# A deep factorization machine on one core: TensorE signals the use of gates once per job and each tile once when it is begun

## The reference, cut to what matters

```python
sp_emb = emb_tables[fidx, sp_input]           # 2048 samples x 26 fields, rows of 32 out of 26 tables of 12500 rows
lin_vals = lin_tables[fidx, sp_input, 0]      # one more value per lookup
lin_output = ds_input @ lin_w.T + lin_b + jnp.sum(lin_vals, axis=1, keepdims=True)
s = jnp.sum(sp_emb, axis=1)
bi_pooled = 0.5 * (s * s - jnp.sum(sp_emb * sp_emb, axis=1))
x = jnp.concatenate([bi_pooled, ds_input], axis=1)      # 2048 x 45
h = jax.nn.relu(x @ w1.T + b1)                          # 45 -> 256
h = jax.nn.relu(h @ w2.T + b2)                          # 256 -> 128
out = jax.nn.sigmoid(h @ fw.T + fb + lin_output)
```

## Time and profile before

| | |
|---|---|
| time before, 3 runs | 456.66, 459.72, 461.10 us, median 459.72 |
| span of the profiled execution, first to last instruction | 459.0 us (its own time beside the span is not shown) |
| TensorE matmuls busy | 406.9 us (89%) |
| VectorE busy | 331.9 us (72%) |
| GpSimd busy | 283.8 us (62%) |
| ScalarE busy | 258.8 us (56%) |

### The profile page before, as it was taken

How to read it: one execution, slowest core, us unless ns; L and a number is a source line. 1 busy time by engine, 2 the same in 40 slices (tenths; PEclk the granted TensorE clock), 3 DMA queues, 4 the chain that set the end, 5 groups by cost and what they waited for, 6 DMA issues and landing times.

```text
span 459.0 us, 5550 instructions
## 1 busy us (share of the span) xinstructions
PE 406.9 (89%) x1798; PEld 335.6 (73%) x1798; DVE 331.9 (72%) x357; ACT 258.8 (56%) x450; POOL 283.8 (62%) x308
## 2 busy tenths in 40 slices
PE   8998989899987989879989799889799866998967
PEld 5787877688776878768768588668588744757734
DVE  7778597976689576956929759649569967587733
ACT  6899645765457544746355564565556745552133
POOL 6675575575755766657557567557566575556740
PEclk9998999899999989999999899999899995999979
DMA  7632253232522226223352233422253121122210
GB/s 208 180 45 23 24 125 67 22 24 12 169 22 23 25 11 168 23 24 25 49 142 12 21 25 62 131 23 12 23 136 50 12 15 10 10 13 12 14 10 0
DMA packets 17126, 23.03 MB, mean 50 GB/s; under 512 B 6246, under 2 KB 16184, under 8 KB 16187
## 3 DMA queue, kind: packets, MB, share of 16 engines
q0 software_dynamic: 9536, 5.05, 19.9%
q1 hardware_dynamic: 7560, 17.62, 12.2%
HBM read 22.61 MB, written 0.04 MB: 49 GB/s over the span
## 4 chain that ended last, share of the span: by engine, by line
PE 36%; issue 33%; another core or an unknown queue 9%; ACT 9%; DVE 7%; DMA 5%; SPq 0%; DVEq 0%; ACTq 0%
PE cand L892 16%; PE cand L895 16%; DMA stage<-tabs 5%; ACT gates L719 3%; ACT distance L711 2%; DVE gates L461 2%; DVE masked L486 2%; DVE low L473 1%; ACT high L686 1%; PE cand L939 1%; PE cand L949 1%; PE bank_b L939 1%; ACT bank_a L705 1%; DVE picks L546 1%
## 5 line engine op out<-in xcount | busy, mean ns | idle before, releaser
L367 POOL DMA_INDIRECT rows<-table,row_idx x293 | 278.0, 949 | 156.5 <-issue 72.9
L892 PE MATMUL cand<-high,gates 128*128 128x462 f32 x826 | 318.8, 386 | 18.9 <-issue 17.8
L895 PE MATMUL cand<-low,gates 128*128 128x462 f32 x826 | 315.0, 381 | 15.3 <-issue 15.1
L892 PEld LDWEIGHTS cand<-high,gates 128*128 128x128 f32 x826 | 160.2, 194 | 54.2 <-issue 33.7
L895 PEld LDWEIGHTS cand<-low,gates 128*128 128x128 f32 x826 | 160.2, 194 | 37.9 <-issue 19.5
L486 DVE TENSOR_TENSOR masked<-cand,mask 128x924 f32<-128x924 f32 x58 | 64.8, 1117 | 89.9 <-remote 87.9
L494 DVE TENSOR_REDUCE picks<-masked 128x66 f32<-128x924 f32 x56 | 107.2, 1914 | 1.9
L719 ACT ACTIVATE gates<-distance,one 128x512 fp32r<-128x512 bf16 (+1 forms) x128 | 83.8, 703 | 12.1 <-remote 12.1
L711 ACT ACTIVATE distance<-codes,minus_key 128x512 bf16<-128x512 f16 (+1 forms) x119 | 77.7, 703 | 0.1
L699 ACT COPY bank_b<-high 128x462 f32<-128x462 f32 x47 | 25.8, 549 | 85.8 <-issue 51.5
L461 DVE TENSOR_SCALAR gates<-bank_a,key_of 128x512 fp32r<-128x512 f32 (+1 forms) x82 | 56.1, 739 | 0.5 <-PE bank_b L986 0.5
(11 more groups left out here) (112 smaller groups left out, 126.1 us busy)
## 6 DMA issues: line engine op xcount, KB each, us to landing
stage<-tabs SPq DMA_DIRECT2D x7, 1617.0 KB
rows<-table,row_idx POOLq DMA_INDIRECT x293
codes<-codes_dram SPq DMA_DIRECT2D x27, 128.0 KB
stage<-tabs SPq DMA_DIRECT2D x7, 231.0 KB, 2.9
idx_raw<-sparse SPq DMA_DIRECT2D x1, 208.0 KB
w_sb<-w2t SPq DMA_DIRECT2D x1, 128.0 KB
dense_sb<-dense_cols SPq DMA_DIRECT2D x1, 120.0 KB
x_and_y<-dense_rows SPq DMA_DIRECT2D x1, 112.0 KB
```

The lines of the kernel that those rows point to most:

```text
L367: pool.indirect_dma_start(out=to, out_offset=None, in_=table[:, :], in_offset=bass.IndirectOffsetOnAxis(ap=row_idx[:, at:at + 1], axis=0), ...
L892: first = nc.tensor.matmul(to, gate, high[f % 2][:, k, :], start=(k == 0), stop=False)
L895: last = nc.tensor.matmul(to, gate, low[f % 2][:, k, :], start=False, stop=(k == CHUNKS - 1))
```

## The change

`gates_used` is incremented once per job, by the low matmul of chunk 6 of the job's last tile, and all who wait for it count jobs. VectorE waits for it once ahead of a job's gates and ScalarE with each gate as before, both for the end of job `j - 3`. `half_tile_begun` becomes `tile_begun`, incremented at chunk 0 of each tile, and the table of gathers has one entry per tile in place of two; an entry is the sum of the two entries that it replaces. In the rest of the kernel nothing changes.

```diff
-    HALVES = (0, 4)
     AHEAD = 400
-    LET_OF = [[30, 30, 30, 440, 40, 40, 40, 340]] + [[135, 101] * TB] * (NJ - 5) + [[175] * 8, [175] * 8, [150] * 8, [280] * 4]
+    LET_OF = [[30, 30, 30, 900]] + [[236] * TB] * (NJ - 5) + [[350] * TB, [350] * TB, [300] * TB, [560] * 2]
...
                     if begun_until(n) > 0:
-                        pool.wait_ge(half_tile_begun, begun_until(n))
+                        pool.wait_ge(tile_begun, begun_until(n))
...
+                if j >= 3:
+                    dve.wait_ge(gates_used, j - 2)
                 for k in range(k0, k1):
                     g = j * CHUNKS + k
-                    if g >= SLOTS:
-                        dve.wait_ge(gates_used, g - SLOTS + 1)
...
-                    dve.wait_ge(gates_used, (j + 1) * CHUNKS)
+                    dve.wait_ge(gates_used, j + 1)
...
-                    dve.wait_ge(gates_used, NJ * CHUNKS)
+                    dve.wait_ge(gates_used, NJ)
...
-                        act.wait_ge(gates_used, FIRST_OF[f - 1] * CHUNKS)
+                        act.wait_ge(gates_used, FIRST_OF[f - 1])
...
-                if g >= SLOTS:
-                    act.wait_ge(gates_used, g - SLOTS + 1)
+                if j >= 3:
+                    act.wait_ge(gates_used, j - 2)
...
-                if k in HALVES:
-                    first.then_inc(half_tile_begun, 1)
+                if k == 0:
+                    first.then_inc(tile_begun, 1)
                 last = nc.tensor.matmul(to, gate, low[f % 2][:, k, :], start=False, stop=(k == CHUNKS - 1))
-                if i == SIZE[j] - 1:
+                if i == SIZE[j] - 1 and k == CHUNKS - 1:
                     last.then_inc(gates_used, 1)
```

More of the change, by code:

```diff
@@ L128, in build_deep_fm @@
     AT_A = {(2, 3): TURN, (2, 6): L1A, (3, 1): L1B, (3, 4): L2}
-    HALVES = (0, 4)
     AHEAD = 400
-    LET_OF = [[30, 30, 30, 440, 40, 40, 40, 340]] + [[135, 101] * TB] * (NJ - 5) + [[175] * 8, [175] * 8, [150] * 8, [280] * 4]
+    LET_OF = [[30, 30, 30, 900]] + [[236] * TB] * (NJ - 5) + [[350] * TB, [350] * TB, [300] * TB, [560] * 2]
     LET = [0] + list(itertools.accumulate(itertools.chain.from_iterable(LET_OF)))
-    assert len(LET) == 1 + sum(SIZE) * len(HALVES)
+    assert len(LET) == 1 + sum(SIZE)
     assert AHEAD + LET[-1] > 100 * sum(GF)
@@ L262, in build_deep_fm @@
         act_gates = sem("act_gates")
-        half_tile_begun = sem("half_tile_begun")
+        tile_begun = sem("tile_begun")
         half_matched = sem("half_matched")
```

## The result

| | before | changed |
|---|---|---|
| median of 20 runs | 460.18 us (456.66 to 464.63) | 464.96 us (460.33 to 473.78) |
| ratio | | 1.0083, 95% interval 1.0056 to 1.0110 |

The change makes the kernel 0.8% slower, about 4 us; on another chip (e18) the ratio was 1.0107. The profiled execution of the changed kernel took 467.59 us, more than its median, so its trace serves for mechanisms, and sizes come from the ratios.

The account below looks back on a forecast made before the run. The prediction took TensorE's 1652 chunk matmuls to set the pace, with 51.5 us of stops and low clock in jobs 1 to 25. Signals, gates and gathers each counted 0: 459.0 - 0 - 0 - 0 = 459 us, range 442 to 469.

Parts of the forecast that it names:

- What bounds the kernel: TensorE's chunk matmuls at 0.21 us each, plus 51.5 us of stops and low clock in jobs 1 to 25.
- slower rival: GpSimd's gathers hold others' signals until it pauses; earlier release lengthens holds: up to 475, likely 467; chance 0.24.
- Signals at 0: On TensorE's chunk matmuls: 298 fewer semaphore increments save 0, at most 0.9 us.
- Gates at 0: VectorE's and ScalarE's new waits for the end of job j - 3 are already met: cost 0.
- Gathers at 0: On GpSimd: 119 gathers let go 4 chunks earlier, 4 in job 0 by 14 to 16; gain at the end 0.
- The faster rivals: TensorE's stops come from its signals, 445, chance 0.26; or each increment costs its own time, 451 to 456, chance 0.12.
- The sum, 459: Whole kernel: profiled span 459.0 with 0 for signals, gates and gathers; own range 456 to 462.
- within 1%: Whole kernel: the outcome class of a time from 455 to 464; chance 0.39.

Follow-up runs that it names:

- e18: The changed kernel itself, run again on another chip: 470.45 us against 465.26 us for the kernel before, ratio 1.0107.
- e7: Kernel before with every second gather of tiles 0 to 14 left out, all TensorE signals kept: 393.65 us, ratio 0.853.
- e12: Kernel before with AHEAD 30000, so no gather waits for TensorE and only the ring of four row buffers holds GpSimd: 620.86 us, ratio 1.348.
- e1: Kernel before with gates_used signalled once per job and its waits counting jobs, gathers still let go per half tile: 461.13 us, ratio 1.0009.
- e3: Kernel before with all 476 signals, only the gather table changed to release by whole tiles as in the changed kernel: 465.80 us, ratio 1.0123.
- e10: Kernel before with tile signals at chunks 0, 2, 4 and 6 and the table split alike, 236 more signals: 460.94 us, ratio 0.9993.
- e2: Kernel before with the tile signal once per tile and the summed table, gates_used still per chunk: 466.18 us, ratio 1.0100.
- e4: Changed kernel with the tile signal at chunk 4 instead of chunk 0 in jobs 1 to 25: median 466.2 us, ratio 1.0014, means of all runs 1.0098.
- e6: Kernel before with the whole-tile gather table in jobs 26 to 29 alone: 464.23 us, ratio 1.0020, means of all runs 1.0054.
- e13: Changed kernel with AHEAD 340 in place of 400, gathers let go later: 468.83 us against 467.03, ratio 1.0059.
- e11: Kernel before with AHEAD 475 in place of 400, gathers let go earlier, still by half tiles: 463.53 us, ratio 1.0055.
- e5: Kernel before with the whole-tile gather table in jobs 0 to 25 alone: 463.57 us, ratio 1.0054.
- e17: Changed kernel with a 256-column GpSimd memset behind each gather, on the same chip as e16: 464.92 us, ratio 0.9950.
- e9: Kernel before with a 256-column GpSimd memset behind each gather: 450.92 us in four runs, ratio 0.9794.
- e16: The kernel of e9 run once more on another chip: 464.75 us, ratio 0.9987.

## Why the prediction was wrong, point by point

- **What bounds the kernel: right in its sum, open in its cause.** The pace of 0.21 us per matmul and 51.5 us of stops and low clock were read correctly. That the stops are not TensorE's own showed in rows 5 to 7, where other engines wait as well; the gathers as their cause were only the slower rival's guess. e7 and e12 show it, in both directions.
- **Signals at 0: right.** e1, e3 and e10 take away 180, keep all, and add 236, and only the table of e3 moves the time. The Trainium skill, page "TensorE: Matmul & The Clock Gate", section "The cost: per-tile semaphore tail", has 26.3 ns for each increment. By that e1 would have given 180 x 26.3 ns = 4.7 us, 1.0%; the interval of e1 excludes more than 0.24%. The page's case, increments of many small matmuls at the end of a packed tile, is not this kernel's.
- **Gates at 0: right** (e1).
- **Gathers at 0: the step that failed.** I asked who needs the rows and found nobody in a hurry, "Gain at the end 0", and did not price what letting a gather go earlier does to the other engines, though the slower rival had named it. The support for 0, that GpSimd "trails its permissions anyway", was a misreading. 2.36 gathers per tile are GpSimd's pace of 1.25 us only in an undisturbed tile of 2.95 us; over the jobs 1 to 25 a tile takes 3.46 us (346.28 by 100), one gather in 1.47 us. So GpSimd catches up with its permissions and waits for them, 53.5 + 27.5 = 81 us in 60 waits, and the table sets when it runs and when it pauses. e3, which moves nothing but the release, puts that term at +1.2% (0.8 to 1.7%), the whole change at +0.8%, 3.8 us.
- **The slower rival: right in kind, wrong in detail and size.** Gathers hold the signals of others, and GpSimd's pause lets them through. But its price came from bursts that grow by a gather. Counted over the starts of all 298 gathers, with a pause where two starts are over 2.5 us apart, runs between pauses did not grow: 27 runs in both kernels, the longest 16 gathers before and 14 after. What grew are the pauses, from 62 to 74 us in all (what each distance has over 1.25 us). In seven kernels with whole tiles in the last jobs (after, e2, e3, e4, e6, e13, e18) they sum to 71 to 74 us, in before, e1, e10 and e11, with half tiles or quarters, to 62 to 63. But e5 has 65 and e11 has 62, and both are 0.5% slower than before, so the pauses are a mark of the change and not the account of its cost. The rival's 467 was about twice the measured loss.
- **The faster rivals: false.** Fewer signals shortened neither the stops (22 of 1.2 us and more, 19 before) nor VectorE's idle time before its pick (86 us, 88 before).
- **The sum, 459,** missed the median of 464.96 by 6 us. The median lies inside the range, but only because the range was stretched over the rivals; the 459's own range of 456 to 462 misses it. The ratio of 1.0083 falls into the class "within 1%" (0.39), for a reason that this class did not have. The mechanism that came true had 0.24, the faster ones 0.38 together: too little and too much against rows 6 and 7, which already pointed away from TensorE's signals.

Open: what in a gather holds the signals (descriptors, their writes or their completions) was not tried, only that it is not a backlog of their packets (e12). Nor is it settled by which chain of waits the other release costs its 4 us, how advance and grain share the loss, or why two chips are 1% slower than the rest. That the cost runs through the held signals is argued, from e7, e12 and e17; that it comes from the release times is shown, by e3.

## What to carry to other kernels

Where one engine issues gathers in long runs, a permission table can be a throttle for the whole core. Changing when a gather may go, even with no gather needed sooner, can change the time of engines that have nothing to do with it; here an earlier release and a coarser one each cost about half a per cent. Before calling such a term 0, compare the pace of the permissions, stops included, with the pace of the engine that waits for them. A matmul's semaphore increments can stay where they are useful, in a kernel like this one. A "remote" wait whose known sender ended long ago is a sign to look at what a third engine does at that time, and to take half of that away in one experiment.

## What the runs showed of the hardware that was not expected

- GpSimd's indirect gathers, 128 rows of 132 bytes each, one in 1.25 us, keep semaphore signals of TensorE from arriving, in e12 one for 74 us. Bursts come through about 2 us after GpSimd stops in the kernel before (2.2 us in job 28) and 2.4 to 4.4 us in e12, but for its first long run of 76 gathers, after which it took 11 us.
- The packets of the gathers are not late meanwhile: 2.0 to 3.8 us from issue to the last packet through that run of e12.
- With gathers 1.44 us apart in place of 1.25 signals are still late (VectorE waits 72.3 us for them in e9, 85.2 in e16), but TensorE's stops are shorter and its clock is 0.985 and 0.967 in place of 0.958.
- During such a hold TensorE goes on at full pace for some us, then issues a matmul every 1.4 us, or every 2.8 us (e12).
- Half of the gathers left out makes the kernel 15% faster, with TensorE 98% busy at a full clock (e7), though the profile gives the queue of the gathers a share of about 20% of the DMA engines.
- The same kernel took 460.4 us on one chip and 467.0 us on another, with a spread of 11 us among 23 runs there.
